# First experts of a transformer kernel: rows scattered onward from pass to pass in place of inverse tables and gathers

## The chip, the cores and the metric

The kernel runs on one core of a Trainium2 chip. A core has five engines that run their own instruction streams and meet at semaphores: TensorE (PE; its weight loads are listed as PEld), VectorE (DVE), ScalarE (ACT), GpSimd (POOL) and SyncE (SP, which here only issues DMAs). 16 DMA engines move the data, whoever issues a transfer. The metric is the time of one execution on the device in microseconds.

## The reference

The reference is two transformer layers in f32 on 8 x 512 tokens of 128 features. The change touches the feed-forward part of layer 0, a mixture of 8 experts of which each token takes two, one after the other:

```
gate_weights = softmax(x @ gate_W + gate_b)
topk_vals, topk_idx = top_k(gate_weights, 2)
boost = x
for i in range(2):
    eo = relu(boost @ W1[e] + b1[e]) @ W2[e] + b2[e]        # e = topk_idx[..., i]
    outs.append(eo)
    if i < 1: boost = boost + 0.5 * eo
fused = topk_vals[0] * outs[0] + topk_vals[1] * outs[1]
x = layernorm(x + layernorm(x + fused) * gamma + beta)
```

So there are two passes over the tokens. In pass 0 a token visits its first expert; in pass 1 the token, with half of the first result added, visits its second. The attention of layer 0 stands before this, and a test-time-training layer and another mixture of experts behind it.

## The kernel before, in words

The kernel is a sequence of blocks. In a block each engine has its own list of instructions, and between two blocks stands a barrier of all five engines: no engine starts the next block before each of them, SyncE too, has come to the end of its list. 4,096 tokens are 32 tiles of 128 rows; `x` holds them in SBUF.

1. `enter_ffn_0` normalizes `x` (class `Norms`: `bn_stats`, then small operations called moments), transposes it into `xT`, loads the weights of the experts, and stores `x` to `x_rows` in DRAM, by four DMAs.
2. `gates_0` makes the gate weights and the two best experts of each token (`hot`, `top`).
3. `places_0` gives every token a slot in each pass. Slots are sorted by expert and each expert's slots are rounded up to whole tiles of 128, so that 40 tiles (`SLOT_TILES`) are always enough and each tile has one expert (`expert`). VectorE counts this out up to `place` (L812). Then the inverse is made: for each slot its source token or slot and its weight. It is a sum of products of one-hot tables, `in_lane` and `what` (L820 to L826), by 64 matmuls a pass (L781), and ends in `source` and `weight` (L837, L838).
4. `experts_0` runs twice. A step is one tile: GpSimd gathers 128 rows by an indirect DMA at `source` (L877) into a ring of 8 buffers; TensorE transposes them (L887), multiplies with W1 (L895), transposes (L905) and multiplies with W2 (L914); ScalarE and VectorE copy, add biases and combine; SyncE stores the 128 result rows in slot order (L987) to `mid_rows` (pass 0: two vectors a slot) or `last_rows` (pass 1). The four TensorE parts of one step belong to four different tiles.
5. `finish_0` gathers the 32 tiles back to token order (L1015, by `home`) and does the two layer norms with reductions and squares, in four groups of 8 tiles.
6. `ttt_layer` loads the next layer's weights (L1783 to L1789) in a block of its own, `transpose_tokens` makes `xT` in another, and then `qkv` begins (L1243).

An indirect DMA is an instruction of GpSimd that moves 128 rows between SBUF and rows of a DRAM table that are named by a list of 128 numbers in SBUF.

## Time and profile before

| | |
|---|---|
| median of 3 runs | 2407.34 us (2403.01 to 2408.51) |
| the profiled execution | 2398.8 us, span 2397.1 us |
| TensorE busy | 1935.5 us (81% of the span) |
| VectorE busy | 1660.8 us (69%) |
| ScalarE busy | 1198.1 us (50%) |
| GpSimd busy | 587.8 us (25%) |
| mean granted TensorE clock | 0.908 of full speed |

The shares are means over stages of different kinds: the attention fills the first 1083 us. The stages that the change touches lie between 1083.7 and 1413.6 us of the span and are best read one by one, by their begin and end in the order of time. "Granted clock" is the share of TensorE's full clock that the chip allowed; 0.5 is 1.2 GHz and 1.0 is 2.4 GHz. Issuing a DMA by SyncE is not counted as busy; in the order of time such a row (SPq) shows how long the issue took, not the transfer.

### The profile page before, as it was taken

Reading aid. Unit: us, or ns where it says so; the run is one execution under the profiler, and the core shown is the slowest. Engines: PE = TensorE matmul, PEld = TensorE weight load, DVE = VectorE, ACT = ScalarE, POOL = GpSimd, SP = SyncE. Lnnn points to the kernel's source line nnn. Section 1 sums busy time; section 2 is a strip of 40 time slices with the busy share of each in tenths; the row PEclk is TensorE's granted clock in tenths of the full one; section 3 lists DMA queues with packets and bytes.
Section 4 is the critical chain, followed back from the end, with each engine's and each line's share of the span. In section 5 each row is a group of like instructions: output and inputs, shape, how many; then the busy total and the mean of one; then the engine's idle time right before and its main releaser. Section 6 shows DMA issues by size and latency. Waiting matters only on the chain. (4 is left out here: it accounts for less than half of the span.)

```text
span 2397.1 us, 35530 instructions
## 1 busy us (share of the span) xinstructions
PE 1935.5 (81%) x11500; PEld 1484.7 (62%) x11500; DVE 1660.8 (69%) x4000; ACT 1198.1 (50%) x2714; POOL 587.8 (25%) x629
## 2 busy tenths in 40 slices
PE   6999999999999999994789142999989998932771
PEld 4777777777777777773667132777767776711761
DVE  5888888888888888875465677677567755557433
ACT  5777777777777777772033232233223322240432
POOL 0111111111111111110345615443133411000372
PEclk9999999999999999995699566999999999965896
DMA  6000000000000000003044100000000000022243
GB/s 205 1 1 1 1 1 1 1 1 1 1 1 1 1 1 1 1 1 99 27 111 115 49 20 0 1 0 0 1 1 0 0 0 3 1 65 71 74 96 84
DMA packets 60472, 62.37 MB, mean 26 GB/s; under 512 B 6560, under 2 KB 50032, under 8 KB 60064
## 3 DMA queue, kind: packets, MB, share of 16 engines
q1 hardware_dynamic: 49936, 43.79, 5.9%
q0 software_dynamic: 10384, 16.66, 3.5%
q8 instruction: 82, 1.34, 0.2%
q14 instruction: 70, 0.57, 0.1%
HBM read 41.36 MB, written 18.81 MB: 25 GB/s over the span
## 5 line engine op out<-in xcount | busy, mean ns | idle before, releaser
L517 DVE TENSOR_TENSOR probT<-turn_ps,probT 128x512 fp32r<-128x512 f32 x512 | 346.5, 687 | 81.3 <-ACT probT L435 72.1
L445 ACT ACTIVATE prob<-prob,negmax 128x512 f32<-128x512 f32 x512 | 371.2, 725 | 60.8 <-DVE negmax L512 56.9
L278 POOL TENSOR_TENSOR x<-x,scaled 128x512 f32<-128x512 f32 x128 | 165.1, 1290 | 897.2 <-DVE scaled L529 897.2
L435 ACT CAST probT<-turn_ps 128x512 fp32r<-128x512 f32 x512 | 297.2, 581 | 127.7 <-PE turn_ps L333 127.7
L512 DVE CUSTOM_DVE_ANT_0 prob<-score_ps,bias 128x512 f32<-128x512 f32 x512 | 332.4, 686 | 1.4 <-issue 1.4
L333 PE MATMUL turn_ps<-ident,prob 128*128 128x128 f32 x2048 | 290.4, 279 | 39.1 <-DVE probT L517 34.5
L333 PEld LDWEIGHTS turn_ps<-ident,prob 128*128 128x128 f32 x2048 | 223.0, 140 | 137.4 <-DVE probT L517 101.8
L345 PE MATMUL ctx_ps<-probT,val 128*128 128x512 f32 x1024 | 270.1, 405 | 0.0
L323 PE MATMUL score_ps<-k,q 64*128 64x512 f32 x1536 | 247.5, 427 | 5.7 <-DVE negmax L512 4.3
L345 PEld LDWEIGHTS ctx_ps<-probT,val 128*128 128x128 f32 x1024 | 177.8, 188 | 61.8 <-issue 23.0
L323 PEld LDWEIGHTS score_ps<-k,q 64*128 64x128 f32 x1536 | 124.6, 185 | 82.4 <-issue 35.0
L1358 POOL TENSOR_TENSOR w<-c,vc 128x512 f32<-128x512 f32 x64 | 82.9, 1295 | 218.2 <-DVE c L1470 218.2
L355 PE MATMUL out_ps<-wo,ctxT 128*128 128x128 f32 x1024 | 135.4, 275 | 0.7 <-ACT ctxT L441 0.7
L1430 ACT CAST dpT_hi<-pred_ps 128x128 fp32r<-128x128 f32 x64 | 17.1, 267 | 232.6 <-PE pred_ps L1377 232.6
L355 PEld LDWEIGHTS out_ps<-wo,ctxT 128*128 128x128 f32 x1024 | 124.8, 192 | 1.2 <-ACT ctxT L441 1.1
L441 ACT COPY ctxT<-ctx_ps 128x512 f32<-128x512 f32 x128 | 75.7, 592 | 54.8 <-PE ctx_ps L345 54.8
L445 ACT ACTIVATION_READ_ACCUMULATOR prob<-prob,negmax 128x1 f32 x512 | 96.9, 189 | 0.0
L529 DVE TENSOR_TENSOR scaled<-out_ps,inv 128x512 f32<-128x512 f32 x128 | 87.4, 683 | 2.7 <-PE out_ps L355 2.7
L1463 DVE TENSOR_TENSOR s<-u_ps,sg 128x512 f32<-128x512 f32 x64 | 44.3, 692 | 55.6 <-ACT sg L1435 55.6
L939 ACT COPY xgT<-x_ps 128x128 f32<-128x128 f32 x80 | 21.3, 266 | 109.0 <-PE x_ps L887 96.7
L1398 PEld LDWEIGHTS dwp_ps<-dp,h 128*128 128x128 f32 x512 | 67.0, 191 | 5.9
L150 PE MATMUL tt<-ident,x 128*128 128x128 f32 x32 | 6.5, 396 | 79.0 <-PEq L1778 79.0
(489 smaller groups left out, 4095.5 us busy)
## 6 DMA issues: line engine op xcount, KB each, us to landing
ew<-L_ffn_fc_weight SPq DMA_DIRECT2D x32, 256.0 KB
bias<-bias_line SPq DMA_DIRECT2D x16, 448.0 KB, 9.5
mid_rows<-row SPq DMA_DIRECT2D x40, 128.0 KB
last_rows<-row SPq DMA_DIRECT2D x40, 64.0 KB
rows_dram<-rows SPq DMA_DIRECT2D x1, 2304.0 KB, 18.6
acc_dram<-zero POOLq DMA_DIRECT2D x1, 2112.0 KB, 16.9
acc<-acc_dram SPq DMA_DIRECT2D x4, 528.0 KB
x_rows<-x SPq DMA_DIRECT2D x4, 512.0 KB, 6.1
```

Of the source, the lines that this page charges most:

```text
L278: pool.tensor_tensor(mine, mine, scaled[a][:, :, :], ALU.add).then_inc(added, 1)
L323: mm = pe.matmul(score_ps[a][:, :], q[p][u][head(a), tile_of(i)], k[p][v][head(a), :], start=(n == 0), stop=(n == 2))
L333: mm = pe.transpose(turn_ps[g % 2][:, tile_of(t)], prob[p][a][:, t, tile_of(c)], ident[:, :])
L345: mm = pe.matmul(ctx_ps[:, :], val[r // 2 % 2][:, c, r % 2 * 2 + a, :], probT[n][:, c, :], start=(c == 0 and n == 0), stop=(c == QT - 1 an ...
L355: mm = pe.matmul(out_ps[:, tile_of(t)], ctxT[a][:, tile_of(t)], wo[:, 2 * r + a, :], start=True, stop=True)
L435: act.copy(probT[0][:, g % QT, :], turn_ps[g % 2][:, :]).then_inc(turned_hi, 1)
L441: act.copy(ctxT[a][:, :], ctx_ps[:, :]).then_inc(ctx_ready, 1)
L445: act.activation(prob[p][a][:, i, :], prob[p][a][:, i, :], ACT.Exp, bias=negmax[p][:, i, a:a + 1], scale=-1.0, accum_out=total[p][:, i, a: ...
L512: dve.tensor_tensor_reduce(prob[p][a][:, i, :], score_ps[a][:, :], bias[:, h, first:first + SEQ][:, ::-1], -1.0, 3.0e38, ALU.add, ALU.min, ...
L517: dve.tensor_tensor(probT[1][:, g % QT, :], turn_ps[g % 2][:, :], probT[0][:, g % QT, :].bitcast(F32), ALU.subtract).then_inc(turned_lo, 1)
L529: dve.tensor_tensor(scaled[a][:, :, :], out_ps[:, :].rearrange("p (t d) -> p t d", t=QT), inv[r % 4][:, :, a:a + 1].to_broadcast([P, QT, D ...
L1358: pool.tensor_tensor(w[r][:, :], c1[p][:, :], vc[p][:, :], ALU.mult).then_inc(w_ready, 1)
```

## The change

The tables in DRAM now are `a_rows` (by the slots of pass 0), `b_rows` (by the slots of pass 1) and `home_rows` (by token). Each row carries, behind its vector or vectors, the numbers that the rest of its way needs: `a_rows` the weight of pass 0, the target slot in pass 1, the weight of pass 1 and the token; `b_rows` the weight of pass 1 and the token. Between them rows are scattered by indirect DMA: 32 tiles of `x` from `places_0` into `a_rows`, 40 tiles from pass 0 into `b_rows`, 40 from pass 1 into `home_rows`. A pass loads its rows in slot order by plain DMAs of SyncE. Slots that no token takes are visited too, so `a_rows` and `b_rows` are first filled: zeros in the body and spare targets in the tail. The inverse tables and their matmuls go. A step of a pass is now two tiles (G = 2, 20 steps), each with its own expert. `finish_0` loads the ordered rows, makes both norms by `bn_stats` and moments, transposes into `xT` as the tiles come, and loads the next layer's weights (`load_ttt`); `ttt_layer` no longer does either.

```diff
-            def store(g):
-                if g < LAST:
-                    sp.wait_ge(by_act, G * (g + 1))
-                else:
-                    sp.wait_ge(by_dve, G)
-                sp.dma_start(keep["x_rows"].rearrange("(t p) d -> p t d", p=P)[:, norms.of(g), :], x[:, norms.of(g), :]).then_inc(x_out, 16)
...
+            sp.wait_ge(empty_ready, 4)
+            a_rows, b_rows = (keep[k].rearrange("(j p) w -> p j w", p=P)[:, 0:SLOT_TILES, :] for k in ("a_rows", "b_rows"))
+            sp.dma_start(a_rows[:, :, 0:D], zero[:, 0:D].unsqueeze(1).to_broadcast([P, SLOT_TILES, D])).then_inc(keep["a_cleared"], 16)
+            sp.dma_start(a_rows[:, :, D:], tail_a[:, :, :]).then_inc(keep["a_cleared"], 16)
             sp.dma_start(w1[:, :, :], ins["L0_ffn_W1"].rearrange("e d h -> d e h")).then_inc(w_in, 16)
             sp.dma_start(w2[:, :, :], ins["L0_ffn_W2"].rearrange("e (f p) d -> p (e f) d", p=P)).then_inc(w_in, 16)
-            store(0)
             sp.dma_start(flat(b1[:, :, :]), ins["L0_ffn_b1"].rearrange("e h -> (e h)").partition_broadcast(P)).then_inc(w_in, 16)
-            store(1)
             sp.dma_start(flat(b2[:, :, :]), ins["L0_ffn_b2"].rearrange("e d -> (e d)").partition_broadcast(P)).then_inc(w_in, 16)
             sp.dma_start(gamma[:, :], ins["L0_ffn_ln_gamma"].partition_broadcast(P)).then_inc(w_in, 16)
-            store(2)
             sp.dma_start(beta[:, :], ins["L0_ffn_ln_beta"].partition_broadcast(P)).then_inc(w_in, 16)
-            store(LAST)
+            sp.dma_start(b_rows[:, :, 0:2 * D], zero[:, :].unsqueeze(1).to_broadcast([P, SLOT_TILES, 2 * D])).then_inc(keep["b_cleared"], 16)
+            sp.dma_start(b_rows[:, :, 2 * D:], tail_b[:, :, :]).then_inc(keep["b_cleared"], 16)
...
+            number = lambda out, base: pool.iota(out, pattern=[[P, SLOT_TILES]], base=base, channel_multiplier=1, allow_small_or_imprecise_dtypes=True)
+            pool.memset(zero[:, :], 0.0)
+            pool.memset(tail_a[:, :, :], 0.0).then_inc(empty_ready, 1)
+            pool.memset(tail_b[:, :, :], 0.0).then_inc(empty_ready, 1)
+            pool.wait_ge(empty_ready, 2)
+            number(tail_a[:, :, 1], SPARE)
+            number(tail_a[:, :, 3], N_TOK).then_inc(empty_ready, 1)
+            number(tail_b[:, :, 1], N_TOK).then_inc(empty_ready, 1)
...
-            for i in range(R):
-                pool.wait_ge(tiled, i + 1)
-                pool.tensor_tensor(what[i][:, :, 1, :], in_tile[i][:, :, :], top[:, i, :].unsqueeze(2).to_broadcast([P, TILES, S]),
-                                   ALU.mult).then_inc(weighed, 1)
+            iota(tile_no[:, :], [[1, K]], 0)
+            iota(x_row[:, :, D + 3], [[P, TILES]], 1)
+            pool.wait_ge(keep["a_cleared"], 32)
+            pool.wait_ge(copied, COPIES + 2)
+            pool.wait_ge(placed, 2)
+            for t in range(TILES):
+                pool.indirect_dma_start(out=keep["a_rows"], out_offset=bass.IndirectOffsetOnAxis(ap=home[:, t:t + 1], axis=0),
+                                        in_=x_row[:, t, :], in_offset=None).then_inc(sent, 16)
+            pool.wait_ge(sent, 16 * TILES)
...
-                for t in range(TILES):
-                    mm = pe.matmul(flat(back_ps[i][:, :, :]), in_lane[i][:, t, :], flat(what[i][:, t, :, :]),
-                                   start=(t == 0), stop=(t == TILES - 1))
-                mm.then_inc(turned_back, 1)
-                pe.wait_ge(turned_back, 2 * i + 2)
...
+            act.copy(x_row[:, :, D], top[:, 0, :]).then_inc(copied, 1)
+            act.copy(x_row[:, :, D + 2], top[:, 1, :]).then_inc(copied, 1)
+            for c in range(COPIES):
+                tiles = slice(c * TILES // COPIES, (c + 1) * TILES // COPIES)
+                act.copy(x_row[:, tiles, 0:D], x[:, tiles, :]).then_inc(copied, 1)
...
+            dve.tensor_copy(home[:, :], place[:, 0, :]).then_inc(placed, 1)
+            dve.tensor_copy(x_row[:, :, D + 1], place[:, 1, :]).then_inc(placed, 1)
...
-    G, F, ROW_RING, X_RING = PAIR, H_0 // P, 4, 8
-    GROUPS = SLOT_GROUPS
+    BASE = 0 if i == 0 else D
+    WEIGHT, TARGET = (D, D + 1) if i == 0 else (2 * D, 2 * D + 1)
+    G, F, RING = 2, H_0 // P, 6
+    GROUPS = SLOT_TILES // G
...
+        @block.sync
+        def _(sp):
+            for n in range(GROUPS):
+                if n >= RING:
+                    sp.wait_ge(row_ready, n - RING + 1)
+                    sp.wait_ge(target_ready, n - RING + 1)
+                    if i == 0:
+                        sp.wait_ge(rest_ready, n - RING + 1)
+                sp.dma_start(xg[n % RING][:, :, :], table.rearrange("(j p) w -> p j w", p=P)[:, G * n:G * (n + 1), :]).then_inc(loaded[n % RING], 16)
...
+            for m in range(GROUPS):
+                r = m % RING
+                pool.wait_ge(target_ready, m + 1)
+                pool.wait_ge(row_ready, m + 1)
+                if i == 0:
+                    pool.wait_ge(rest_ready, m + 1)
                 for g in range(G):
-                    k = G * n + g
-                    pool.indirect_dma_start(out=xg[r][:, g, :], out_offset=None, in_=table,
-                                            in_offset=bass.IndirectOffsetOnAxis(ap=source[:, i, k:k + 1], axis=0)).then_inc(gathered[r], 16)
+                    pool.indirect_dma_start(out=result, out_offset=bass.IndirectOffsetOnAxis(ap=target[r][:, g:g + 1], axis=0),
+                                            in_=row[r][:, g, :], in_offset=None).then_inc(sent[r], 16)
+            for r in range(RING):
+                pool.wait_ge(sent[r], 16 * G * ((GROUPS - 1 - r) // RING + 1))
...
+            def carry_on(m):
+
+                r = m % RING
+                act.wait_ge(loaded[r], 16 * visit(m))
+                if m >= RING:
+                    act.wait_ge(sent[r], 16 * G * (m // RING))
+                act.copy(target[r][:, :], xg[r][:, :, TARGET]).then_inc(target_ready, 1)
+                if i == 0:
+                    act.copy(row[r][:, :, 2 * D:], xg[r][:, :, D + 2:]).then_inc(rest_ready, 1)
...
+                    last = dve.scalar_tensor_tensor(row[r][:, g, at:at + D], y[m % 2][:, g, :], xg[r][:, g, WEIGHT:WEIGHT + 1],
+                                                    xg[r][:, g, BASE:BASE + D], ALU.mult, ALU.add)
...
+        @block.sync
+        def _(sp):
+            for g in range(GROUPS):
+                sp.dma_start(f[:, of(g), :], keep["home_rows"].rearrange("(t p) d -> p t d", p=P)[:, of(g), :]).then_inc(fetched[g], 16)
+            load_ttt(core, ins, keep, sp)
...
+                pool.tensor_tensor(plus[:, of(g), :], x[:, of(g), :], along(beta), ALU.add).then_inc(plus_ready, 1)
...
+            def shape(g):
+                dve.wait_ge(by_inner, G * (g + 1))
+                dve.tensor_tensor(f[:, of(g), :], f[:, of(g), :], along(gamma), ALU.mult).then_inc(shaped, 1)
+                dve.wait_ge(shaped, g + 1)
+                dve.wait_ge(plus_ready, g + 1)
+                dve.tensor_tensor(f[:, of(g), :], f[:, of(g), :], plus[:, of(g), :], ALU.add).then_inc(summed, 1)
+
+            for s in range(GROUPS + 2):
+                if s < GROUPS:
+                    dve.wait_ge(fetched[s], 16)
+                for k in range(G):
+                    if s < GROUPS:
+                        dve.bn_stats(inner.raw[:, s * G + k, :], f[:, s * G + k, :]).then_inc(inner.seen, 1)
+                    if s >= 2:
+                        outer.moments(dve, s - 2, k)
+                if 1 <= s <= GROUPS:
+                    shape(s - 1)
+                    dve.wait_ge(summed, s)
+                for k in range(G):
+                    if 1 <= s <= GROUPS:
+                        t = (s - 1) * G + k
+                        dve.bn_stats(outer.raw[:, t, :], f[:, t, :]).then_inc(outer.seen, 1)
+                    if s < GROUPS:
+                        inner.moments(dve, s, k)
+            dve.wait_ge(outer.shift_ready, GROUPS)
+            for t in range(HALF, TILES):
+                dve.tensor_scalar(x[:, t, :], f[:, t, :], outer.inv[:, 0, t:t + 1], outer.shift[:, t:t + 1], ALU.mult, ALU.add).then_inc(by_dve, 1)
+            dve.wait_ge(turn_done, CHUNKS)
+            dve.tensor_copy(xT[:, (CHUNKS - 1) * 512:], flat(bank[CHUNKS - 1][:, :, :]))
...
+                for k in range(G):
+                    if k == G // 2 and s >= 2:
+                        outer.root(act, s - 2)
+                    if s <= GROUPS:
+                        inside((s - 1) * G + k)
...
+                    if 0 <= t < HALF:
+                        outside(t)
...
-        transpose_tokens(core, keep["x"], keep["xT"], keep["ident"])
```

On SyncE, in the entry block (its end is the branch) and the first DMAs behind it. `w` and `b` are the experts' weights and biases; a name in "waits" is the one that the semaphore's number bore at its first use. Before:

```order
19 L1114 DMA w_101<-L_ffn_W 128x8x256
20 L1115 DMA w_102<-L_ffn_W 128x16x128
21 L1110 DMA x_rows<-x 128x8x128 [waits inv_ready_72]
22 L1117 DMA b_103<-L_ffn_b 128x2048
23 L1110 DMA x_rows<-x 128x8x128 [waits inv_ready_72]
24 L1119 DMA b_104<-L_ffn_b 128x1024
25 L1120 DMA gamma<-L_ffn_ln_gamma 128x128
```

and now:

```order
19 L1093 DMA a_rows<-zero 128x40x128 [waits line_copied_23]
20 L1094 DMA a_rows<-tail_a 128x40x4
21 L1095 DMA w_107<-L_ffn_W 128x8x256
22 L1096 DMA w_108<-L_ffn_W 128x16x128
23 L1097 DMA b_109<-L_ffn_b 128x2048
24 L1098 DMA b_110<-L_ffn_b 128x1024
25 L1099 DMA gamma<-L_ffn_ln_gamma 128x128
26 L1100 DMA beta<-L_ffn_ln_beta 128x128
27 L1101 DMA b_rows<-zero 128x40x256
28 L1102 DMA b_rows<-tail_b 128x40x2
29 L1080 UNCONDITIONAL_BRANCH
30 L811 UNCONDITIONAL_BRANCH [waits barrier_Pool_Activation_PE_DVE_SP_release]
```

The stores of `x` are gone; the filling of `a_rows` stands ahead of the weights and that of `b_rows` behind them, as the last issue before the barrier.

On GpSimd, from the constants of `places_0` to the first rows of pass 0. Before:

```order
165 L751 IOTA tile_no 128x40
166 L767 TENSOR_TENSOR what_185<-in_tile_183,top 128x32x40
167 L767 TENSOR_TENSOR what_186<-in_tile_184,top 128x32x40
168 L730 UNCONDITIONAL_BRANCH
169 L867 UNCONDITIONAL_BRANCH
170 L877 DMA xg_198<-x_rows,source 128x128
```

and now:

```order
168 L712 IOTA tile_no 128x40
169 L712 IOTA x_row 128x32
170 L727 DMA a_rows<-x_row,home 5120x132 x32
171 L695 UNCONDITIONAL_BRANCH
172 L821 UNCONDITIONAL_BRANCH
173 L832 DMA b_rows<-row_200,target_206 10240x258 x2
```

The 32 indirect DMAs stand in the block of `places_0`, ahead of the barrier; those of a pass follow its results in place of leading them.

## Rows read from the trace of the kernel before

**Rows 1.** Busy time by stage; the first line names the columns.
```profile
core 0: us, PE busy (x) PEld busy (x) DVE busy (x) ACT busy (x) POOL busy (x), PEclk, DMA share, GB/s
1176.50:1254.30 77.80, 65.67 (x360) 49.38 (x360) 48.49 (x160) 25.31 (x80) 38.25 (x40) 0.94 0.38 103
1329.90:1401.40 71.50, 0.00 (x0) 0.00 (x0) 51.73 (x61) 20.87 (x49) 36.01 (x32) 0.50 0.11 30
```

**Rows 2.** The order of time at stage ends: start, length, engine, line, tiles, wait before.
```profile
1102.15 1.28 ACT L684 ACT_TABLE_LOAD   x1 [1.89 <-PEq L1096]
...
1133.39 1.01 DVE L812 TENSOR_REDUCE place<-slot 128x64 f32<-128x512 f32 x1
...
1176.54 1.16 POOL L877 DMA_INDIRECT xg<-x_rows,source  x1 [23.18 <-POOLq L730]
...
1179.27 0.48 PE L887 MATMUL x_ps<-ident,xg 128*128 128x128 f32 x1 [4.53 <-DMA xg<-x_rows,source]
```

**Rows 3.** DMA issues of SyncE in order of time, around large transfers.
```profile
3.31 0.86 SPq L96 DMA_DIRECT2D x<-L_attn_hidden_states  x1
...
8.14 3.34 SPq L98 DMA_DIRECT2D bias_line<-line  x1
...
2144.42 0.59 SPq L2006 DMA_DIRECT2D rows_dram<-rows  x1
...
2151.12 7.68 SPq L2009 DMA_DIRECT2D ew<-L_ffn_fc_weight  x1
```

**Rows 4.** DMA issues by tile: count, KB, us from issue to landing.
```profile
rows_dram<-rows SPq DMA_DIRECT2D x1, 2304.0 KB, 18.6
...
x<-L_attn_hidden_states SPq DMA_DIRECT2D x1, 0.5 KB, 11.9
```

**Rows 5.** Three short stretches, columns as in the first group.
```profile
5.00:7.00 2.00, 2.00 (x3) 0.14 (x1) 0.00 (x0) 0.00 (x0) 0.00 (x0) 1.00 1.00 399
...
2148.00:2158.00 10.00, 2.23 (x6) 1.73 (x6) 7.78 (x36) 0.00 (x0) 0.00 (x0) 0.50 1.03 290
...
1179.20:1187.20 8.00, 6.82 (x25) 4.96 (x26) 1.94 (x6) 1.99 (x7) 5.71 (x6) 0.55 0.19 50
```

**Rows 6.** Indirect DMAs of GpSimd: by line (busy, mean ns), then in time.
```profile
L877 POOL DMA_INDIRECT xg<-x_rows,source x40 | 38.3, 956 | 50.2 <-POOLq L730 23.2 <-DVE row L967 17.7 <-issue 9.4
...
L2282 POOL DMA_INDIRECT acc_dram<-ey,slots x32 | 51.2, 1600 | 23.2 <-issue 7.9 <-DVE ey L2398 7.7 <-DMA acc_dram<-ey,slots 7.6
...
2347.16 1.55 POOL L2282 DMA_INDIRECT acc_dram<-ey,slots  x1 [0.30 <-issue]
...
2350.74 1.55 POOL L2282 DMA_INDIRECT acc_dram<-ey,slots  x1 [2.02 <-DMA acc_dram<-ey,slots]
```

**Rows 7.** The order of time within the passes and at their ends.
```profile
1192.12 0.30 PE L887 MATMUL x_ps<-ident,xg 128*128 128x128 f32 x1
...
1193.65 0.30 PE L887 MATMUL x_ps<-ident,xg 128*128 128x128 f32 x1
...
1251.16 0.34 DVE L967 SCALAR_TENSOR_TENSOR row<-y,weight,xg 128x128 f32<-128x128 f32 x1
...
1257.11 0.47 PE L887 MATMUL x_ps<-ident,xg 128*128 128x128 f32 x1 [6.62 <-DMA xg<-mid_rows,source]
...
1327.54 0.35 DVE L967 SCALAR_TENSOR_TENSOR row<-y,weight,xg 128x128 f32<-128x128 f32 x1
...
1329.95 4.42 DVE L1043 TENSOR_TENSOR plus<-x,beta 128x4096 f32<-128x4096 f32 x1 [2.06 <-PEq L851]
```

**Rows 8.** By line: two operations of the normalizations (busy, mean ns).
```profile
L1134 DVE BATCH_NORM_STATS2 norm_raw<-x 128x6 f32<-128x128 f32 x32 | 7.8, 279 | 2.5 <-PEq L58 2.5
...
L1058 DVE TENSOR_TENSOR f<-f,gamma 128x1024 f32<-128x1024 f32 x4 | 4.9, 1226 | 0.1
```

**Rows 9.** The order of time: eight tiles normalized, and the next layer's start.
```profile
1090.16 3.18 ACT L632 ACTIVATE x<-x,norm_shift,norm_inv 128x128 f32<-128x128 f32 x8
...
1413.57 0.67 PE L1243 MATMUL qk_ps<-qkv_w,xT 128*128 128x256 f32 x2 [1.05 <-PEq L139]
```

More of the change, by code:

```diff
@@ L846, in experts_0 @@
-    source, weight, expert = keep["source"], keep["weight"], keep["expert"]
-    table, result = (keep["x_rows"], keep["mid_rows"]) if i == 0 else (keep["mid_rows"], keep["last_rows"])
+    w1, w2, b1, b2, ident, expert = (keep[k] for k in ("w1", "w2", "b1", "b2", "ident", "expert"))
+    table, result = (keep["a_rows"], keep["b_rows"]) if i == 0 else (keep["b_rows"], keep["home_rows"])
     IN_W, OUT_W = table.shape[1], result.shape[1]
-    G, F, ROW_RING, X_RING = PAIR, H_0 // P, 4, 8
-    GROUPS = SLOT_GROUPS
+    BASE = 0 if i == 0 else D
@@ new lines, in add_rows @@
+            def add_rows(m, e):
+                r = m % RING
+                dve.wait_ge(y_done, m + 1)
+                for g in range(G):
+                    dve.tensor_tensor(y[m % 2][:, g, :], y_ps[m % 2][:, g * D:(g + 1) * D], b2[:, bass.ds(e[g], 1), :].rearrange("p a d -> p (a d)"),
+                                      ALU.add).then_inc(y_ready, 1)
+                if m >= RING:
+                    dve.wait_ge(sent[r], 16 * G * (m // RING))
+                dve.wait_ge(y_ready, G * (m + 1))
@@ L1007, in finish_0 @@
         block = st.enter_context(nc.Block())
-        tiles = [slice(g * G, (g + 1) * G) for g in range(GROUPS)]
-        by_token = lambda v, g: v[:, tiles[g]].unsqueeze(2).to_broadcast([P, G, D])
-        along = lambda v, n: v[:, :].unsqueeze(1).to_broadcast([P, n, D])
+        of = inner.of
+        along = lambda v: v[:, :].unsqueeze(1).to_broadcast([P, G, D])
+        LAST, HALF = GROUPS - 1, TILES - G // 2
+        @block.sync
[3 more added lines that the diff above has]
+            load_ttt(core, ins, keep, sp)
@@ L1087, in _, with inside, outside, copy_chunk @@
-            act.wait_ge(finished, TILES)
+            def inside(t):
+                inner.apply(act, f, t).then_inc(by_inner, 1)
+            def outside(t):
+                act.activation(x[:, t, :], f[:, t, :], ACT.Identity, bias=outer.shift[:, t:t + 1], scale=outer.inv[:, 0, t:t + 1]).then_inc(by_act, 1)
+            def copy_chunk(c):
+                act.wait_ge(turn_done, c + 1)
+                act.copy(xT[:, c * 512:(c + 1) * 512], flat(bank[c][:, :, :]))
+            inner.warm_up(act)
@@ new lines, in _ @@
+            act.wait_ge(outer.eps_ready, 2)
+            inner.root(act, 0)
+            for s in range(1, GROUPS + 2):
+                if s <= GROUPS:
+                    act.wait_ge(inner.shift_ready, s)
+                for k in range(G):
+                    if k == G // 2 and s >= 2:
+                        outer.root(act, s - 2)
+                    if s <= GROUPS:
+                        inside((s - 1) * G + k)
+                if s >= 2:
+                    act.wait_ge(outer.shift_ready, s - 1)
+                for k in range(G):
+                    if k == G // 2 and s < GROUPS:
+                        inner.root(act, s)
+                    t = (s - 2) * G + k
+                    if 0 <= t < HALF:
+                        outside(t)
+                if s == 1:
+                    continue
+                if s >= 3:
+                    for c in (2 * (s - 3), 2 * (s - 3) + 1):
+                        copy_chunk(c)
@@ L1090, in enter_ffn_0, with _ @@
+            copy_chunk(CHUNKS - 2)
+        @block.tensor
+        def _(pe):
+            for c in range(CHUNKS):
+                pe.wait_ge(by_act, min(4 * (c + 1), HALF))
+                if 4 * (c + 1) > HALF:
+                    pe.wait_ge(by_dve, 4 * (c + 1) - HALF)
+                for j in range(4):
+                    mm = pe.transpose(bank[c][:, j, :], x[:, 4 * c + j, :], ident[:, :])
+                mm.then_inc(turn_done, 1)
 def enter_ffn_0(core, ins, keep, gamma, beta):
```

319 lines of the change are left out of this document (97 added, 222 removed).

## Prediction

> **What bounds the kernel now.** I read the table of stages first. All of the change lies between 1083.7 and 1413.6 us; before it runs the attention, behind it the test-time-training layer, and neither is edited. The stage rows [rows 1] show the two kinds of stage. In a pass of the first experts (77.8 us) TensorE is busy 65.7 us: it sets the pace. In the finishing stage (71.5 us) TensorE does nothing, VectorE is busy 51.7 us and GpSimd 36.0 us: a serial chain. The order of time at the stage ends [rows 2] gives the anchors: gates start at 1102.15, the slot numbers (`place`) end at 1134.40, the first gather is issued at 1176.54, the first expert matmul starts at 1179.27. Stages are parted by a barrier of all engines, SyncE among them, so a stage ends with its last engine. That is the key to this change: its new DMAs can hold a stage although no engine computes.
>
> **Entry: clearing the new tables.** Three things are new on SyncE: bodies of `a_rows` (5,120 rows of 512 B), their tails (5,120 pieces of 16 B), and the same for `b_rows` (5,120 rows of 1 KB, 5,120 pieces of 8 B). Each transfer is split over 16 DMA engines, so 320 pieces each. Prices: near 2150 the DMA engines moved 290 GB/s of 528 to 576 B rows [rows 5], so about 544 x 16 / 290 = 30 ns a row on an engine; at 5 to 7 us they moved 399 GB/s of longer rows, which for 1 KB makes 41 ns.
> - bodies of a: 320 x 30 = 9.6 us
> - tails of a: no row shows 16 B pieces. From below, extending 41 and 30 ns down the size gives some 15 ns, 5 us; from above I take twice the 30 ns, 19 us. I take 28 ns, 9.0 us, since a fixed cost per piece is what the 512 B rows are nearest to.
> - the weights between them, 3.6 MB with mixed rows at 350 GB/s: 10.5 us
> - bodies of b: 320 x 41 = 13.1 us
>
> From the first byte at about 1086.3 (GpSimd fills the sources first, about 1 us) these end at 1128.5. Does SyncE wait for that? Behind the 2 MB `x` load, issued at 3.31 and landed 11.9 later at 15.2, the next issue lasted 3.34 us, to 11.5; behind `rows_dram`, landed at 2163.0, one issue lasted 7.68 us, to 2158.8, and its forerunner had got free at 2151.1 [rows 3, 4]. So SyncE is let go 4 to 12 us before a large transfer ahead of it lands. The last issue here is the tail of b, behind the body of b. With 6 us SyncE is free at 1122.5, and with 0.8 us for the barrier the gates start at 1123.3 in place of 1102.15: **+21.2 us**. Bounds: 0 if the issues are taken up at once, +42 with tails at 60 ns (+10), 1 KB rows at 290 GB/s (+5) and SyncE held to the end (+6). The stores of `x_rows` that go away were under the computing and give nothing. The rest of the clearing (some 15 us) runs beside gates and slot numbers.
>
> The Trainium skill ("DMA: Bandwidth & Descriptors", Specifications) says that under 512 B the DMA engine does a read-modify-write. No run here shows it for the 16 B tails. If that doubles a 512 B row's price, the sum is the one with 60 ns above.
>
> **Slot numbers: the turn tables go, 32 scatters come.** Removed: what lies between `place` at 1134.40 and the barrier before 1176.54 [rows 2], some 41 us of VectorE comparisons and 128 matmuls that wait for them. Added: two casts (0.4 us), then 32 indirect DMAs, one after the other on GpSimd, whose landing the stage awaits. A gather costs GpSimd 0.956 us [rows 6] plus 0.30 between two, 1.255 us; an accumulating scatter costs 1.600 [rows 6]. The new ones are scatters without accumulating. I take the gather's price, because the two differ from the dear ones by the addition as well as by the direction; the dear price is a rival. 31 x 1.255 + 0.95 = 39.9 us from 1135.0, to 1174.9; landing 2.0 (the wait of 2.02 on an earlier scatter [rows 6]), barrier 1.0, then a load issued by SyncE, 2.6 us to TensorE's first matmul: 1180.5 for 1179.27, **+1.2 us**. ScalarE's copies of `x` lie beside VectorE's chain, which takes some 12 us up to `place`.
>
> **The passes.** Matmuls are the same: a tile takes 1.53 us at full clock (1192.12 to 1193.65 [rows 7]), 40 tiles 61.2. The first pass takes 72.2 us from the first matmul to the last row (1179.27 to 1251.50). About 4 of these are the half clock of the first 8 us (granted 0.55 [rows 5]), 7 are ends and stalls. Pairs of tiles give every engine twice the slack between two waits of TensorE; VectorE's work for a pair is about 2.8 us under TensorE's 3.06. The fill is 1 us longer, stalls shrink by some 3: **-2 us** a pass, between +3 and -5. GpSimd needs 2 x 1.255 = 2.5 a pair, under 3.06, so it keeps up. At a pass's end the last two scatters (2.5), their landing (2.0), the barrier (1.0) and the load (2.6) make 8.1 us; now 1251.50 to 1257.11 are 5.6 [rows 7]: **+2.5**. Behind the second pass 5.5 for the present 2.06 (1327.89 to 1329.95 [rows 7]): **+3.4**. Sum of the passes +1.9.
>
> **Finish.** From 1329.95 to the first matmul of the next layer at 1413.57 are 83.6 us [rows 7, 9]. The 32 gathers, the two-pass mean and variance, the separate loads and the separate transposes go. New: SyncE loads 512 KB of ordered rows (about 4.5 us to the first), then VectorE and ScalarE alternate by groups of eight tiles. ScalarE applies eight tiles in 3.2 us [rows 9]; a statistics instruction lasts 0.28 us and overlaps the next, 2.2 us with the moments between them; `gamma` and `plus` are 1.23 us each [rows 8]. Per steady group: ScalarE's rest of the last group 2.2, eight inner tiles with a root 3.5, VectorE's shaping 2.5, statistics to the variance 1.5, root and shift 0.9, makes 10.6 us. In order: first group 7.8, then 8.1, 9.4, 10.6, 9.9 and a tail of 5.9 (last statistics, eight tiles, two transposed chunks, one copy), 51.7 us, and 1.2 for the barrier: 52.9. **-30.7 us**; bounds -24 (GpSimd's additions slow VectorE) and -38 (groups overlap fully). The weights of the next layer load under it.
>
> **Sum.** +21.2 +1.2 +1.9 -30.7 = -6.4 us. The profiled execution took 2398.8 us (span 2397.1), so it would take 2392.4. The median of the three runs, 2407.34, lies 8.5 higher; on it 2401 us.
>
> **Rivals.**
> - *Scatters are dear* (slower). If a plain scatter costs 1.57 + 0.30 = 1.87 us, the stage of slot numbers grows by 32 x 0.62 = 20 us, and GpSimd needs 3.74 a pair against TensorE's 3.06: each pass then takes about 40 x 1.87 + 11 for the first rows + 3 = 89 in place of some 78, twice +11. -6.4 + 20 + 22 = +36, about 2443. For it: the only scatters in the trace cost that. Against: they also add, which needs a second read. It decides from 1.53 us a scatter on in the passes, and from 1.45 the whole is no longer faster.
> - *Clearing is dearer* (slower). Tails at 60 ns or more, or slow 1 KB stores: +4 to +15, about 2415. Its place is SyncE's last issue of the entry stage.
> - *SyncE is not held.* If the issues are taken up at once, gates start at 1102 and all is -28: 2380. For it: `rows_dram` itself was taken up in 0.59 us, though it is as large [rows 3]. Against: what came behind it was held, and here the large ones come one behind another. But then the b clears collide with the 32 scatters, which could give back some 5.
> - *The finish gains little* because ScalarE's and VectorE's turns don't overlap: 60 in place of 51.7, total +2, 2409.
>
> **Chances.** My forecast (within 8 us around -6) 45%, dear scatters 18%, dearer clearing 17%, SyncE not held 14%, small finish 6%. A difference within 0.2% (4.8 us) can hardly be told from none. Faster by more: about half of the forecast's cases and all of the unheld ones and a few of the others, 0.43; within, 0.20; slower, 0.37. The range from 2376 to 2446 holds the dear scatters and the unheld SyncE; the likeliest case alone spans 2390 to 2411.
>
> **What would show it.** In the changed trace: SyncE's last two issues of the entry stage are long, and the gates start near 1123; GpSimd's 32 scatters have a pitch of 1.25 us (1.87 in the rival); TensorE's wait for the second pass is about 8 us; the finish to the next layer's first matmul is 53 us. I am wrong if the gates start at 1102, if a scatter lasts over 1.2 us, or if a pass lasts outside 75 to 83 us.

## The result, and the profile after

The changed kernel took 2426.7 us (median of 4, 2424.8 to 2428.6), the kernel before 2406.3 beside it: **1.0091 times**, 95% interval 1.0075 to 1.0107, so 20 us slower where I had forecast 6 faster. Run again later, the ratio was 1.0104 (1.0090 to 1.0118).

The timeline of the changed kernel, at the places of [rows 2, 3, 7 to 9] (start, duration, engine, line, operation; in brackets the idle time and what ended it):

```profile
1085.86 0.33 SPq L1089 DMA_DIRECT2D gw<-L_ffn_gate_W  x1
1087.02 0.38 SPq L1093 DMA_DIRECT2D a_rows<-zero  x1
1087.45 8.39 SPq L1094 DMA_DIRECT2D a_rows<-tail_a  x1
1104.38 6.78 SPq L1097 DMA_DIRECT2D b<-L_ffn_b  x1
1112.70 0.43 SPq L1101 DMA_DIRECT2D b_rows<-zero  x1
1113.18 17.13 SPq L1102 DMA_DIRECT2D b_rows<-tail_b  x1
1130.72 1.28 ACT L652 ACT_TABLE_LOAD   x1 [28.31 <-PEq L1080]
1130.76 13.79 PE L646 MATMUL logit_ps<-gw,xT 128*128 128x8 f32 x64 [27.95 <-PEq L1080]
1166.37 1.17 POOL L727 DMA_INDIRECT a_rows<-x_row,home  x1 [12.14 <-DVE x_row L775]
1167.84 0.97 POOL L727 DMA_INDIRECT a_rows<-x_row,home  x1 [0.30 <-issue]
1206.05 0.97 POOL L727 DMA_INDIRECT a_rows<-x_row,home  x1 [0.31 <-issue]
1211.42 2.92 SPq L819 DMA_DIRECT2D xg<-a_rows  x6
1213.70 0.69 PE L844 MATMUL x_ps<-ident,xg 128*128 128x128 f32 x2 [56.02 <-DMA xg<-a_rows]
...
1288.30 0.61 DVE L943 SCALAR_TENSOR_TENSOR row<-y,xg 128x128 f32<-128x128 f32 x2
1292.88 0.97 POOL L832 DMA_INDIRECT b_rows<-row,target  x1 [0.30 <-issue]
1299.45 2.92 SPq L819 DMA_DIRECT2D xg<-b_rows  x6
1302.30 0.69 PE L844 MATMUL x_ps<-ident,xg 128*128 128x128 f32 x2 [15.09 <-DMA xg<-b_rows]
...
1381.64 0.97 POOL L832 DMA_INDIRECT home_rows<-row,target  x1 [0.30 <-issue]
1387.65 1.28 ACT L593 ACT_TABLE_LOAD   x1 [13.58 <-PEq L794]
1441.27 1.19 PE L1230 MATMUL qk_ps<-qkv_w,xT 128*128 128x256 f32 x2 [2.17 <-PEq L58]
```

The first line is the begin of the entry block. Before, the same line stood at

```profile
1083.71 0.33 SPq L1112 DMA_DIRECT2D gw<-L_ffn_gate_W  x1
```

Read them as anchors. The entry begins at 1085.86 (1083.71 before). The gates start at 1130.72 (1102.15 before), the first pass at 1213.70 (1179.27), the second at 1302.30 (1257.11), the finish at 1387.65 (1329.95), the next layer at 1441.27 (1413.57). The differences of neighbours give the table:

| stage, us | before | after | change | forecast |
|---|---|---|---|---|
| attention (not edited), to the entry | 1083.71 | 1085.86 | +2.2 | 0 |
| entry, to the gates' start | 18.4 | 44.9 | +26.4 | +21.2 |
| gates and slot numbers | 77.12 | 82.98 | +5.9 | +1.2 |
| first pass to its last row / boundary behind | 72.2 / 5.6 | 75.2 / 13.4 | +3.0 / +7.8 | -2 / +2.5 |
| second pass / boundary | 70.8 / 2.1 | 74.6 / 10.7 | +3.8 / +8.7 | -2 / +3.4 |
| finish, to the next layer's first matmul | 83.6 | 53.6 | -30.0 | -30.7 |
| sum | | | +27.7 | -6.4 |

The rest of the span adds 1.8: 2426.6 for 2397.1. That is 29.5 where the medians differ by 20.4, since the profiled execution of before (2398.8) was faster than any of its four timed ones and that of after was the slowest of its four. In two profiles from one chip (before_again, after_again) the difference is 17.5: +2.3 for the attention, +26.3, +3.5, +7.9 and +8.3 (a pass with its boundary), -29.9, and -0.9 for the rest. So the attention's +2.2 is the spread between executions: over the runs below the entry block begins anywhere from 1083.6 to 1089.2.

**Entry.** Windows of the entry (length, busy time of each engine, granted clock, DMA share, GB/s), to set beside [rows 5]. The last two run from the end of the small tail pieces to the last piece of the bodies of `b_rows`:

```profile
1087.00:1097.00 10.00, 3.85 (x15) 2.65 (x16) 7.79 (x53) 7.86 (x23) 0.00 (x0) 0.50 1.03 234
1097.00:1103.00 6.00, 4.76 (x19) 3.07 (x17) 3.88 (x13) 4.73 (x12) 0.00 (x0) 0.50 1.61 62
...
1104.30:1118.90 14.60, 0.00 (x0) 0.00 (x0) 0.00 (x0) 0.00 (x0) 0.00 (x0) 0.50 0.93 260
1118.90:1136.70 17.80, 5.95 (x28) 5.98 (x29) 0.00 (x0) 1.28 (x1) 0.14 (x1) 0.50 1.15 291
```

From 1104.3 to 1130.7 no engine computes. SyncE is held in two issues: a bias load from 1104.38 to 1111.16, and its last one, the tail of `b_rows`, from 1113.18 to 1130.31. The DMA engines are busy in all four windows (share 0.9 and more), even at 62 GB/s, while the 16 B tails pass.

**A stall in a pass.** The same trace from 1227 to 1231.1, one of about six such places in each pass:

```profile
1227.02 1.06 PE L871 MATMUL y_ps<-w,hT 128*128 x8
1227.95 0.97 POOL L832 DMA_INDIRECT b_rows<-row,target  x1 [0.43 <-issue]
1228.20 0.41 PE L844 MATMUL x_ps<-ident,xg 128*128 128x128 f32 x2
1229.40 0.60 PE L862 MATMUL t_ps<-ident,hs 128*128 128x128 f32 x4
1231.00 0.37 ACT L895 COPY xgT<-x_ps 128x256 f32<-128x256 f32 x1 [3.01 <-remote]
1231.07 0.29 DVE L934 TENSOR_TENSOR y<-y_ps,b 128x128 f32<-128x128 f32 x1 [2.60 <-PE y_ps L871]
```

TensorE wrote `y_ps` from 1227.02 and `x_ps` from 1228.20, yet VectorE, which waits for the one, and ScalarE, which waits for the other, both go on only at 1231.0. The trace's own record of the two semaphores, which this view leaves out, has their updates at 1230.93 and 1230.98; one group earlier each came 0.01 us behind the end of its matmuls. TensorE meanwhile went on with other matmuls. Whether its results or only its signals were late the trace can't say, since the ends of matmuls in it are modelled; below I call it late signals. A group of two tiles takes 2.8 us, and at about every third group 2 to 3 more.

### The profile page after: what moved, and what is told of

It is laid out like the page before. It is cut to its first block and busy times, and to the rows that moved or that the text cites. A ratio compares the mean times of both kernels' runs of the same rounds, so it can differ in the third digit from the quotient of the medians.

```text
span 2426.6 us, 35057 instructions
## 1 busy us (share of the span) xinstructions
PE 1909.0 (79%) x11372; PEld 1464.9 (60%) x11372; DVE 1612.1 (66%) x4034; ACT 1199.7 (49%) x2724; POOL 590.0 (24%) x640
## 5 line engine op out<-in xcount | busy, mean ns | idle before, releaser
L413 ACT ACTIVATE prob<-prob,negmax 128x512 f32<-128x512 f32 x512 | 371.1, 725 | 61.6 <-DVE negmax L480 57.5
L485 DVE TENSOR_TENSOR probT<-turn_ps,probT 128x512 fp32r<-128x512 f32 x512 | 346.6, 688 | 81.3 <-ACT probT L403 72.1
L409 ACT COPY ctxT<-ctx_ps 128x512 f32<-128x512 f32 x128 | 75.7, 591 | 55.0 <-PE ctx_ps L313 55.0
L927 DVE TENSOR_TENSOR hs<-h_ps,b 128x256 f32<-128x256 f32 x80 | 30.4, 420 | 97.3 <-PE h_ps L852 80.7
L844 PE MATMUL x_ps<-ident,xg 128*128 128x128 f32 x80 | 18.2, 314 | 81.3 <-DMA xg<-a_rows 56.0
L895 ACT COPY xgT<-x_ps 128x256 f32<-128x256 f32 x40 | 14.9, 374 | 113.7 <-PE x_ps L844 93.8
## 6 DMA issues: line engine op xcount, KB each, us to landing
bias<-bias_line SPq DMA_DIRECT2D x16, 448.0 KB, 11.4
a_rows<-zero SPq DMA_DIRECT2D x1, 2560.0 KB, 13.9
```

The source lines that it names most:

```text
L409: act.copy(ctxT[a][:, :], ctx_ps[:, :]).then_inc(ctx_ready, 1)
L413: act.activation(prob[p][a][:, i, :], prob[p][a][:, i, :], ACT.Exp, bias=negmax[p][:, i, a:a + 1], scale=-1.0, accum_out=total[p][:, i, a: ...
L485: dve.tensor_tensor(probT[1][:, g % QT, :], turn_ps[g % 2][:, :], probT[0][:, g % QT, :].bitcast(F32), ALU.subtract).then_inc(turned_lo, 1)
```

## The experiments

Each ran beside the kernel before on its chip; the kernels that ran together in this way make one occasion. **Which occasion a kernel ran on mattered more than I had thought**: where the kernel before took 2399 to 2406 us, the two-tile passes with scatters show these stalls, and where it took 2388 none do. It isn't the chip alone: the record gives one chip for bursts to early_clears (2388.0) and for stores_first and early_clears_2 (2399.2). So only ratios and stages of one occasion are compared. The changed kernel itself never ran on an occasion without stalls; the nearest to it there is short_pause. The table has the time from a pass's first matmul to its last row, and behind the slash the wait to the next stage:

| kernel | before beside it | ratio | gates start | to first pass | pass 1 | pass 2 |
|---|---|---|---|---|---|---|
| clears_later | 2401.0 | 1.0013 [1.0004, 1.0023] | 1104.0 | 88.3 | 75.7 / 13.1 | 71.7 / 10.1 |
| one_tile | 2401.0 | 1.0033 [1.0023, 1.0042] | 1128.2 | 82.7 | 69.9 / 10.0 | 69.9 / 7.7 |
| no_scatters | 2401.0 | one look | 1130.7 | 82.8 | **58.2** / 3.2 | 74.5 / 8.0 |
| both | 2401.0 | 0.9949 [0.9933, 0.9966] | 1103.4 | 90.1 | 70.2 / 9.9 | 71.0 / 7.2 |
| bursts | 2388.0 | one look | 1128.8 | 82.4 | 67.7 / 11.1 | 67.1 / 9.0 |
| spaced | 2388.0 | one look | 1128.8 | 83.0 | 61.8 / 17.5 | 58.7 / 15.6 |
| stores | 2388.0 | one look | 1130.9 | 82.9 | 61.6 / 6.2 | 59.4 / 2.2 |
| early_clears | 2388.0 | 0.9931 [0.9915, 0.9948] | 1104.6 | 82.5 | 68.1 / 10.0 | 66.6 / 7.7 |
| short_pause | 2388.5 | one look | 1130.6 | 82.9 | 60.6 / 13.9 | 59.2 / 11.0 |
| fours | 2388.5 | one look | 1130.3 | 82.9 | 60.6 / 16.3 | 59.8 / 13.3 |
| paced | 2388.5 | 0.9922 [0.9906, 0.9939] | 1105.0 | 83.0 | 61.2 / 13.8 | 59.1 / 11.7 |
| paced_short | 2388.5 | 0.9913 [0.9896, 0.9929] | 1107.6 | 82.9 | 61.3 / 13.9 | 59.8 / 11.0 |
| after_again | 2399.2 | 1.0104 [1.0090, 1.0118] | 1133.7 | 82.7 | 74.2 / 12.6 | 71.1 / 10.1 |
| short_pause_2 | 2399.2 | 1.0118 [1.0102, 1.0133] | 1129.2 | 82.9 | 73.7 / 13.3 | 74.3 / 9.2 |
| early_two | 2399.2 | 0.9989 [0.9976, 1.0001] | 1103.2 | 82.9 | 77.2 / 11.4 | 72.0 / 9.5 |
| before_again | 2399.2 | one look | 1105.1 | 79.3 | 73.4 / 5.5 | 70.9 / 2.1 |
| stores_first | 2399.2 | one look | 1104.8 | 81.3 | **61.5** / 5.7 | 73.1 / 11.0 |
| early_clears_2 | 2399.2 | 0.9918 [0.9904, 0.9932] | 1102.4 | 82.6 | 68.9 / 9.9 | 68.2 / 7.7 |

**clears_later.**
```diff
 # enter_ffn_0, sync:  the four dma_starts into a_rows and b_rows go
+# places_0, sync:     the same four stand here
```


> The four clears of the scatter tables are issued by SyncE in the block of the slot numbers, where it has no work, in place of the block of entry. Theory (the clears hold SyncE, and SyncE holds the barrier behind entry): the gates start near 1103 in place of 1130.7, the time from there to the first matmul of the first pass stays at 83 us, passes and finish stay as they are, and the kernel takes 2426.7 - 28 = 2399 us (2396 to 2404). Rival (the clears cost the same wherever they are, since the scatters then have to share the DMA engines with them): GpSimd's 32 scatters or the wait ahead of them grow by 15 us or more, and the kernel takes 2412 us or more.

The gates start at 1104, so the hold was the clears' alone. But 5.3 us come back: SyncE's clear of the first table, now late, holds the scatters, in this timeline by 18.9 us of idle GpSimd in place of 12.1:

```profile
1125.26 7.91 SPq L715 DMA_DIRECT2D a_rows<-tail_a  x1
1144.71 1.18 POOL L736 DMA_INDIRECT a_rows<-x_row,home  x1 [18.91 <-DMA a_rows<-tail_a]
```

The ratio to the kernel before falls by 0.0078, some 19 us. The profile's span falls by 26.8; of the other 8, 4 are which execution was profiled on either side, and 4 that the kernel before, too, took 5 us less on this occasion. The rival is wrong in its size, right in its direction.

**one_tile, both.**
```diff
-    G, F, RING = 2, H_0 // P, 6
+    G, F, RING = 1, H_0 // P, 8
```


> The passes work tile by tile (G = 1, eight buffers) in place of two tiles at a time (six buffers of two). Theory A (the stalls of 2.7 us at every third group come of the two-tile steps): they shrink to about 1 us as in the kernel before, from the first matmul of a pass to its last row takes 72 us in place of 75, the queue of scatters behind the last row is shorter by about 3 us in each pass, and the kernel takes 2426.7 - 12 = 2415 us (2410 to 2419). Theory B (the stalls are the price of scatters that run beside the passes, whatever the grouping): the last row comes no earlier, and with 40 steps of register loads in place of 20 the kernel takes 2427 us or more.

> Clears in the block of the slot numbers and passes tile by tile. If the two edits are independent the gain is the sum of the gains of the two runs of one edit: 28 + 12 us, so 2387 us, which would be faster than the kernel before (2406). If theory B holds for the passes: 2399 us.

Beside clears_later on the same occasion (75.7 and 71.7) a pass gets 6 and 2 us shorter, with fewer stalls, and its boundary 3 shorter, since fewer scatters stand behind the last row (the last ends 2.3 us behind it, for 4.9). Theory A holds on this occasion, and both edits together beat the kernel before by 0.5%.

**no_scatters.**
```diff
-            for m in range(GROUPS):
+            for m in range(GROUPS if i else 0):
...
```
(the waits for these scatters go too, and the finish loads from `b_rows`)


> Leaves out the first pass's 40 scatters; the second pass reads the cleared rows, scatters them as before, and the finish fetches cleared rows. So the first pass runs without scatters and the second with them, in one execution. Theory B (scatters cause the stalls): the first pass's last row comes 5 to 8 us earlier (67 to 70 us behind its first matmul in place of 75.2), with no stall over 1.5 us at the groups 2, 5, 8, 11, 16. Theory A (two-tile steps): the stalls stay where they are, the last row still comes at 75 us. Either way the wait from the last row to the second pass's first matmul, 13.4 us with scatters, falls to 4 to 6 us, which is the share of scatters in that boundary (7 to 9 us).

The windows of its two passes, and of the two of the changed kernel:

```profile
1213.44:1271.59 58.15, 55.34 (x360) 47.78 (x360) 42.47 (x140) 22.80 (x80) 0.00 (x0) 0.95 0.18 44
1274.81:1349.34 74.53, 58.67 (x360) 48.52 (x360) 36.14 (x120) 20.11 (x60) 36.60 (x38) 0.94 0.33 98
```
```profile
1213.70:1288.91 75.21, 60.39 (x360) 49.96 (x360) 42.99 (x140) 22.01 (x80) 36.22 (x36) 0.91 0.31 95
1302.30:1376.91 74.61, 59.21 (x360) 49.05 (x360) 36.30 (x120) 20.22 (x60) 34.22 (x36) 0.93 0.32 96
```

TensorE's work is the same 360 matmuls; the pass without scatters is 17 us shorter: TensorE is idle for 2.8 us in place of 14.8, and its matmuls last 5 us less at a granted clock of 0.95 for 0.91. Two-tile steps alone, then, don't stall: theory B is right on what it takes. And the boundary falls by 10.2 us, more than I had given the scatters there; the part on boundaries below says where it went.

**bursts, spaced, stores.** GpSimd's loop in turn: two tiles at every second step; a memset behind each scatter; plain stores.
```diff
+                    pool.memset(pause[:, G * m + g, :], 0.0)      # spaced: 128x256
-                    pool.indirect_dma_start(out=result, ...)
+            sp.dma_start(result[...G * m:G * (m + 1)...], row[m % RING])   # stores
```


> As one_tile (tile by tile, eight buffers), but GpSimd scatters two tiles back to back at every second tile, as it does with two-tile steps. Theory C (two scatters back to back are what lets the signals of TensorE arrive some 3 us late): the stalls are back, one of about 2.5 us per six tiles, and a pass takes 74 to 76 us from its first matmul to its last row in place of 69.9. Theory D (it is the two-tile step: half as many hand-overs, each with longer queues behind it, so that a late scatter is felt by all engines): the pass stays at 69 to 71 us.

> As the changed kernel (two-tile steps, six buffers), with a memset of 128x256 on GpSimd behind each scatter, so that scatters are at least 1.5 us apart in place of 1.27. Theory C: the 2.7 us stalls are gone, GpSimd's pace sets the pass (40 x 1.5 = 60 us and its lead-in of 11), 68 to 72 us to the last row. Theory D: the stalls stay, and the slower GpSimd makes the pass no shorter: 75 to 79 us.

> As the changed kernel, but each pass stores its rows slot by slot by plain DMAs of SyncE in place of GpSimd's scatters by target (so no row is sent to its next place). The same bytes are written by as many rows, without GpSimd's indirect instruction. If the traffic of the writes makes the stalls, they stay and the pass takes 73 us or more; if GpSimd's indirect instruction makes them, the pass takes 58 to 62 us, as the first pass without scatters did (58.2). The wait from the last row to the next pass's first matmul: 13.4 us with scatters, 3.2 us without; 5 to 7 us with plain stores, as in the kernel before (5.6), if the backlog and the landing of the scatters make the rest.

None of the three has a stall, and I took the pause for the cure. **That was wrong**: the next four hint at it, after_again shows it. What stands is the price of GpSimd's pace at a boundary (spaced, pitch 1.47 us: 17.5 us) and of plain stores there (6.2).

**short_pause, fours, paced, paced_short.** A memset of 128x16; four tiles back to back; early clears with a memset of 128x176 or of 128x16.


> As the changed kernel, with a memset of 128x16 behind each scatter: it costs GpSimd about 0.1 us, so that scatters can still follow each other at about 1.27 us. In spaced (128x256, pitch 1.47 us) the stalls were gone. Theory E (the pitch is what counts: scatters closer than DVE's pace of 1.4 us a tile come in bursts and delay TensorE's signals): the stalls stay, 74 to 76 us from the first matmul to the last row. Theory F (an instruction of another kind between two scatters is what counts): the stalls are gone at the old pitch, 58 to 62 us, and the wait to the next pass stays at 12 to 14 us.

> As the changed kernel, but GpSimd waits for two groups of two tiles and then scatters four tiles back to back. The mean rate is the same, the bursts are twice as long. Theory E: stalls at least as many as before, 75 us or more to the last row. If longer bursts with a rest behind them do no harm (as pairs with a rest did in bursts: 67.7 us with single-tile steps), 60 to 66 us.

> Two-tile steps, the first table cleared in the block of the gates and the second in the block of the slot numbers, and a memset of 128x176 behind each scatter of the first 16 of 20 groups, which makes the pitch about 1.38 us (1.47 with 256 columns), just under VectorE's 1.4 us a tile. If pacing removes the stalls also there, a pass takes 60 us to its last row and the wait behind it 11 us: 71 us against 78 in early_clears, 7 us twice, and 0.9931 x before falls to about 0.987 (2357 us where the kernel before takes 2388). If only a pitch above 1.4 us helps, the passes take 75 us and the ratio is 0.997 or more.

> As paced, with the memset of 128x16 behind every scatter in place of 128x176. By theory F 0.986 of the kernel before; by theory E the passes keep their stalls (75 us to the last row, 13 behind it) and the ratio is 0.999 to 1.001, which is then also the price of the early clears with two-tile steps and nothing else.

No stall in any, even with the longest bursts: no theory of mine on the pattern of scatters parts them, which pointed to the occasion. In short_pause, the changed kernel with hardly an edit, the time is 2394.5 for 2388.5 before (one look): without stalls the change is about even with before, 0.25% behind.

**after_again, short_pause_2, early_two, before_again**, all on one chip.


> The changed kernel once more. If the stalls belong to the kernel (scatters in an unpaced two-tile pass), they are there again: 75 us from a pass's first matmul to its last row, and 1.009 x the kernel before. If they belong to the chip or the execution that was profiled first, a pass takes 60 to 62 us on a chip without them, and the kernel is at 1.000 to 1.006 x the kernel before, of which the clears are 28 us and the boundaries 15.

> The memset of 128x16 behind each scatter, beside after_again on the same chip. If the pause removes stalls: 15 us less per pass than after_again and a ratio to it near 0.988. If it does nothing: the same time as after_again within 3 us.

> Both tables cleared while slots are worked out, two-tile steps, no pause: after_again less 26 us (28 for entry, less 2 for what comes in its place). If stalls come with unpaced scatters it is 0.998 to 1.000 x the kernel before, and behind paced and paced_short (0.992); if they come with the chip it is at 0.991 to 0.993 on a chip without them.

> The kernel before once more, for its profile on this chip: its passes took 72.2 and 70.8 us to the last row, with pauses of about 1 us at every fourth tile. If such pauses come with the chip, on one without them its passes take 62 to 66 us, and the gap between the two kernels is set by entry, boundaries and finish alone.

The stalls are there with the pause and without. The windows of short_pause, then of short_pause_2, the same kernel:

```profile
1213.55:1274.18 60.63, 55.92 (x360) 47.75 (x360) 42.27 (x140) 22.82 (x80) 40.82 (x71) 0.96 0.39 118
1288.03:1347.21 59.18, 55.85 (x360) 47.83 (x360) 35.68 (x120) 20.93 (x60) 38.67 (x71) 0.95 0.39 120
```
```profile
1212.01:1285.75 73.74, 59.66 (x360) 49.17 (x360) 42.86 (x140) 22.13 (x80) 40.92 (x72) 0.92 0.32 97
1299.05:1373.30 74.25, 60.62 (x360) 50.66 (x360) 36.29 (x120) 20.05 (x60) 40.28 (x73) 0.89 0.32 97
```

13 to 15 us a pass between two occasions of one kernel. The pause does nothing. before_again had stalls of about 1 us at every second to tenth tile, like the first profile of before. early_two is the changed kernel but for the clears, those of the first table in the block of the gates and those of the second in the block of the slot numbers. Beside after_again it takes 2395.8 for 2423.4 us, 27.6 less, where 26 was expected. This is the price of the clears where they stood, with nothing else changed. It came out at 0.9989 of before, on an occasion with stalls.

**stores_first, early_clears_2.**


> As early_two, but the first pass stores its rows slot by slot with plain DMAs of SyncE in place of GpSimd's scatters (so no row goes to its next place between the passes); the second pass scatters as before. On a chip with stalls: if GpSimd's indirect instruction is needed for them, the first pass takes 60 to 62 us from its first matmul to its last row without a stall and the second 71 to 75 with stalls; if the writes are enough, both have them (70 us or more). On a chip without stalls both take 59 to 62 us and nothing is learned on this.

> Early clears and single-tile steps once more. On a chip with stalls the passes take 70 to 71 us to the last row, as in both and one_tile, and the ratio to the kernel before is 0.992 (0.9949 of both, less 7.5 us for the scatters' earlier start); on a chip without them 67 us and 0.993, as in early_clears.

The windows of stores_first, plain stores in the first pass, scatters in the second:

```profile
1186.12:1247.67 61.55, 56.15 (x360) 47.85 (x360) 42.34 (x140) 22.80 (x80) 0.00 (x0) 0.95 0.41 121
1253.40:1326.49 73.09, 60.27 (x360) 50.66 (x360) 36.39 (x120) 20.21 (x60) 34.07 (x36) 0.91 0.32 97
```

The first moves 121 GB/s against 97, so it isn't the amount of traffic. On such an occasion the stalls need the scatters, GpSimd's indirect instruction with its writes to scattered rows. Why the signals are late then stays open.

**early_clears** is the version that beat the kernel before on both kinds of occasion. (paced and paced_short did as well on the one that they ran on.) The first table is cleared in the block of the gates, the second in that of the slot numbers, and passes go tile by tile.


> As both, with the two clears of the first table issued in the block of the gates and the two of the second in the block of the slot numbers. In both GpSimd's scatters started 8.7 us after the slots were known, held by the first table's clear (SyncE issued it at 1125.9, it landed near 1146). With the first table clear before the slots are known the first matmul of the first pass comes 82.5 us behind the gates' start in place of 90.1: 2389.4 - 7.5 = 2382 us. Against it: if the clears hold the barrier behind the gates, as they held the one behind entry, nothing is gained (2389).

GpSimd's first scatter comes as soon as `x_row` is ready. The lines are from early_clears_2:

```profile
1102.79 7.82 SPq L641 DMA_DIRECT2D a_rows<-tail_a  x1
1125.34 12.44 SPq L721 DMA_DIRECT2D b_rows<-tail_b  x1
1138.04 1.18 POOL L740 DMA_INDIRECT a_rows<-x_row,home  x1 [12.14 <-DVE x_row L788]
```

The same two tails still hold SyncE for 8 and 12 us, but now beside gates that last 22 and slot numbers that last 58. It gives 0.9931 and 0.9918 of before.

## Why the prediction was wrong

Two steps failed by some 11 us each, and either alone would have turned the forecast of -6.4 into a loss of 4: the overlap within the passes, where I had stalls shrink, and the end of the passes, where GpSimd's backlog was too small and the drain of its list was left out. Entry and slot numbers add another 10.

**Entry (+21.2, measured +26.4): mechanism right, size too small.** SyncE was held in its last issues and held the barrier. The 6 us by which I let it go ahead of the bodies of `b_rows` were right: it was free at 1130.31, and their last piece moved at 1136.7. The terms that were mis-sized are two rates. For the 1 KB bodies I took 41 ns a row, 13.1 us, from the stretch at 399 GB/s [rows 5]; they took 17.8, at 291. The other row there, 290, was the nearer one, and I had kept it for the bound. The weights ahead of them took 14.6 us at 260 GB/s, not 10.5 at the 350 I assumed. Against these, the 16 B tails were cheaper than taken, 6.6 us for 9.0. So of the rival "clearing is dearer" the slow 1 KB stores came true and the dear tails didn't. The 2.2 us ahead of the entry are not the change's.

**Slot numbers (+1.2, measured +5.9; +3.5 in the two profiles from one chip).** The scatter's price, my largest doubt, was right: 0.97 us and a pitch of 1.274 for 1.255; the dear-scatter rival falls, and with it its +36. Three small things weren't in the sum. The gates' 64 small matmuls last 13.79 us for 11.63: TensorE stood idle in the hold, and the granted clock was 0.50 through them where before it averaged 0.61. The landing and barrier took 4.40 us (1207.02 to SyncE's load at 1211.42), not 3.0; 2.67 of it is the drain that is told of under the boundaries. The pitch made 0.6.

**Passes (-4 inside, measured +6.8): the overlap failed.** I said that two tiles a step give every engine slack and shrink the stalls by 3. Where the kernel before stalls about 1 us at every second to tenth tile, the changed one stalls 2 to 3 at every third group, and a pass is 3 to 4 us longer in place of 2 shorter. Where there are no stalls a two-tile pass with scatters takes 59 to 62 us, but the kernel before wasn't profiled there, so what the step by itself is worth isn't shown. I had seen stalls in before and put them down as ends and waits of TensorE that slack would cover, without asking what made them. no_scatters and stores_first show that the stalls of the changed kernel need its scatters; why only on some occasions stays open.

**Boundaries (+5.9, measured +16.5): the backlog was half, and one term was missing.** I counted two scatters behind the last row, 2.5 us. The last groups run at 1.3 to 2.1 us, since the steps empty, and GpSimd's pace is 2.55 a group, so four scatters stood in line: 1288.91 to 1293.85, 4.9 us, and 5.7 in the second pass. The landing, 2.0, was about right: the last update of the last scatter's semaphore came 1.8 us behind its instruction's end, 1.3 in the second pass and 1.3 in the slot numbers. What I had at nothing comes then. GpSimd's list ends with a DRAIN, an instruction that the trace records and the views above leave out, and the barrier opens only behind it. It lasts from 1295.90 to 1299.21, 3.31 us; behind the second pass it is 3.32, behind the 32 scatters of the slot numbers 2.67. Every run has the same lengths, on both kinds of occasion, tile by tile or by two, and in the passes without scatters (no_scatters, stores_first, stores) it takes 0.04. Worked out from 2.67 for 32 and 3.31 for 40, my estimate is 83 ns for each scatter of the block. The kernel before has drains of 6.7 and 6.3 us, but its gathers lead the pass, so they ended some 4 us ahead of the last row and cost nothing. The Trainium skill ("Perfetto Trace Analysis", DMA Instruction — SWDGE) says that the profile ends such an instruction when its descriptors are written and not when the data has moved; the trace agrees, with packets of the last scatter moving until 1294.95, 1.1 us behind its instruction's end.

**Finish (-30.7, measured -30.0)** was right, and the rival of a small finish falls. **SyncE not held** falls as well.

So the sum was 34 us off: passes 10.8, boundaries 10.6, entry 5.2, slot numbers 4.7, the attention's 2.2, finish 0.7. All on one side. Where a row gave two prices I had taken the lower (399 GB/s for 290), and the drain had none.

## What to carry to other kernels

A DMA that only prepares a table belongs in a block whose engines are busy for longer than its issue takes, even if it is needed much later: here moving four issues by two blocks was worth some 19 us, and moving the first two of them back by one, clear of the scatters, 6 to 8 more on the profile. A stage that ends on GpSimd scatters pays their backlog at its emptying end, then their landing (1.3 to 1.8 us), then the drain of GpSimd's list (2.7 us behind 32 scatters, 3.3 behind 40), 4.4 to 5.6 us in all from the last scatter's end to the next stage's first load; with tiles handed over one by one the backlog is shorter. And an experiment that seems to cure something must have its control on the same occasion: four kernels without stalls meant nothing until the uncured one ran beside one of them.

## What the runs showed that I had not expected

- On some occasions the signals of TensorE reach VectorE and ScalarE up to 3 us late while GpSimd scatters, on others never: 73 to 75 us against 60 for one kernel's pass. The kernel before takes 2399 against 2388 on the two kinds; that this comes from its own smaller stalls is likely but not shown.
- In passes with indirect DMAs on the occasions with stalls the trace lacks some of TensorE's own semaphore records: of those that its matmuls in the first pass should leave it has 108 of 160 in the kernel before and 73 of 80 in the changed one. In the passes without indirect DMAs (no_scatters, stores_first) it has all, and without stalls all but a few (paced 77 of 80 in its second pass). So lost records and late signals come together, and the kernel before has its share.
- From the last packet of a pass's scatters to the next stage 4.5 us pass in which nothing moves (1294.95 to 1299.45); 3.3 of them are GpSimd's drain.
- 5,120 pieces of 16 B, 80 KB in all, took 6.6 us, about 21 ns each on one of the 16 engines by my estimate, less than a row of 512 B.
- A plain scatter costs GpSimd what a gather does (0.97 us for 0.956), whether its rows have 528, 1032 or 512 B.
